# First attention: router logits taken before the output projection, and a new order of TensorE, ScalarE and GpSimd in each step

## What is computed

```python
x = x + tanh(g_xattn[0]) * xattn0(layernorm(x), ctx, ctx, w_q, b_q, w_k, b_k, w_v, b_v, w_o, b_o)
# first mixture: xn = (x - mu) / sqrt(var + eps) * gamma + beta
logits = xn @ Wg.T + bg            # 8 experts, the best 2 of them per token
x = x + tanh(g_ffn[0]) * (layernorm(x) + sum over 2 experts of w * expert(xn))
```

## Time and profile before

| what | value |
|---|---|
| median of 3 runs | 1355.66 us (1352.38 to 1358.79) |
| the profiled execution | 1369.84 us, its span 1368.0 us |
| mean granted TensorE clock | 0.981 |
| busy in the span | PE 95%, DVE 68%, ACT 58%, POOL 52% |
| chain that ended last | PE 85%, DVE 8%, DMA 3%, ACT 2% |

### The profile page before, as it was taken

One profiled execution on the slowest core, in us unless ns is written; L12 is line 12 of the kernel. 1 busy time (PEld: TensorE's weight loads), 2 busy tenths in 40 slices (PEclk: granted clock), 3 DMA queues, 4 the chain that ended last, 5 costly groups with the idle time before them and its releaser, 6 DMA issues.

```text
span 1368.0 us, 38200 instructions
## 1 busy us (share of the span) xinstructions
PE 1297.2 (95%) x14802; PEld 1154.4 (84%) x14802; DVE 930.5 (68%) x2484; ACT 794.5 (58%) x1761; POOL 712.2 (52%) x708
## 2 busy tenths in 40 slices
PE   6999999998889999999999998999999999899898
PEld 5888888886789999999999986889999998545476
DVE  4788888897576655556556216999999997412287
ACT  4566666663457777777777444666566665332454
POOL 1365656553266877778877024566665652200131
PEclk9999999999899999999999997999999999999999
DMA  6574545463457777776775921541121110499812
GB/s 196 186 246 157 182 146 182 148 202 98 158 178 215 221 227 225 232 227 220 221 224 190 375 80 33 174 164 48 53 60 48 49 41 17 172 429 432 355 56 70
DMA packets 103618, 237.24 MB, mean 173 GB/s; under 512 B 8976, under 2 KB 85904, under 8 KB 91024
## 3 DMA queue, kind: packets, MB, share of 16 engines
q1 hardware_dynamic: 97296, 218.02, 46.3%
q0 software_dynamic: 6144, 16.79, 3.9%
HBM read 173.96 MB, written 60.82 MB: 172 GB/s over the span
## 4 chain that ended last, share of the span: by engine, by line
PE 85%; DVE 8%; DMA 3%; issue 2%; ACT 2%; POOL 0%; SPq 0%; DVEq 0%; ACTq 0%; PEldq 0%; POOLq 0%
PE ps L1542 13%; PE psT L1527 7%; PE ps L598 5%; PE psS L575 5%; PE ps L802 5%; PE ps L750 4%; PE psT L584 4%; PE psS L1527 3%; PE ps L1527 3%; PE ps L611 3%; PE ps L735 2%; PE ps L764 2%; PE ps L674 2%; PE psT L590 2%; PE ps L1780 2%
## 5 line engine op out<-in xcount | busy, mean ns | idle before, releaser
L1495 POOL TENSOR_TENSOR wb_lo<-arena,wb_hi 128x2048 fp32r<-128x2048 f32 x64 | 298.0, 4657 | 104.4 <-ACT wb_hi L1615 104.4
L1542 PE MATMUL ps<-wb_hi,hT_hi 128*128 128x256 f32 x528 | 153.3, 290 | 6.5 <-DVE hT_lo L1668 6.5
L584 PE MATMUL psT<-arena 32*128 32x128 f32 x2048 | 155.3, 286 | 0.0
L1542 PE MATMUL ps<-wb_lo,hT_hi 128*128 128x256 f32 x528 | 148.6, 281 | 0.0
L1542 PE MATMUL ps<-wb_hi,hT_lo 128*128 128x256 f32 x528 | 148.6, 281 | 0.0
L575 PE MATMUL psS<-arena 32*128 32x256 f32 x1024 | 143.2, 397 | 0.7 <-ACT arena L963 0.7
L1615 ACT CAST wb_hi<-arena 128x1024 fp32r<-128x1024 f32 x128 | 130.6, 1044 | 6.5 <-DMA arena<-w_dram 6.2
L1169 POOL TENSOR_TENSOR arena<-arena,eps_sb 128x1 f32<-128x1 f32 x96 | 26.2, 273 | 203.2 <-DVE arena L1043 115.4
L584 PEld LDWEIGHTS psT<-arena 32*128 32x128 f32 x2048 | 129.2, 188 | 2.6 <-issue 1.8
L1680 DVE TENSOR_TENSOR arena<-ps,arena 128x512 f32<-128x512 f32 (+1 forms) x39 | 25.4, 650 | 120.1 <-PE ps L1542 79.7
L1542 PEld LDWEIGHTS ps<-wb_hi,hT_hi 128*128 128x128 f32 x528 | 100.3, 190 | 6.8 <-issue 6.7
(11 more groups left out here) (385 smaller groups left out, 3894.4 us busy)
## 6 DMA issues: line engine op xcount, KB each, us to landing
arena<-wset_dram SPq DMA_DIRECT2D x24, 2048.0 KB, 15.5
xs_rows<-arena SPq DMA_DIRECT2D x33, 1024.0 KB, 8.2
arena<-w_dram SPq DMA_DIRECT2D x32, 1028.0 KB, 6.0
arena<-w_dram SPq DMA_DIRECT2D x32, 1024.0 KB, 5.9
arena<-w_dram SPq DMA_DIRECT2D x7, 2052.0 KB, 12.9
w_sb<-xs_rows SPq DMA_DIRECT2D x33, 256.0 KB, 2.7
xs_rows<-arena SPq DMA_DIRECT2D x33, 256.0 KB, 5.5
arena<-ctxT_dram SPq DMA_DIRECT2D x63, 128.0 KB, 2.4
```

What stands on the lines that cost most here:

```text
L584: nc.tensor.matmul(psT[:, b, j * P:(j + 1) * P], kbd[p, (k - 1) % 3, c, par, :], qT[p, (k - 1) % 3, c, :], start=j == 0, stop=False, skip_ ...
L1495: nc.gpsimd.tensor_tensor(wb_lo[:, u % 2, part], wb_raw[:, u % 2, part], wb_hi[:, u % 2, part], ALU.subtract).then_inc(w_g.sem, 1)
L1542: last = nc.tensor.matmul(ps[5][:, t * D:(t + 1) * D], hp[:, f, t * P:(t + 1) * P], wp[:, f, :], start=f == 0 and t == 0 and n == 0, stop= ...
```

## The change

1. **Logits without xn on TensorE.** The logits are linear in x apart from the row's mean and spread. The gate weights, times gamma, are centred over the columns (`wc`), so that the mean drops out. The part of the old x comes from a product of the turned xh (xT) with `wc` (8 columns), made behind Q; ScalarE scales it by the row's spread (`lg_x`), and GpSimd adds a constant row. The part of the attention's output comes with the output product, whose weights `wo_wide` have the 8 columns of w_o times `wc` behind the 256. VectorE adds the two (`lg_sum`) and scales by xn's factor a step later. The turn of xn, its copy by ScalarE and its product go.
2. **Setting up.** TensorE forms the column sums of the scaled gate weights before the first keys, the gate through the transposed output weights (a new load of 256 KB, `oT`) and the constant row in step 2. The gate weights are loaded with the first constants, and scaled by VectorE at once.
3. **The next input first.** The turn of xh of tile k+1 moves from behind the rank product to behind the first score half, and ScalarE copies it ahead of the keys. Q then waits for the copied values, since they share a PSUM bank.
4. **Residual's affine part.** Its two factors are made by GpSimd (from VectorE), and the pass over x by ScalarE (from VectorE), ahead of its copy of aT.
5. **Scatters a tile apart.** The first scatter of tile k-4 is issued ahead of the context parts, the second at the start of the next step, behind a wait for the transposed scores' first half.
6. In the second attention the late contexts are waited for one at a time; the bias addition to x on GpSimd moves one step later.

```diff
+        wo_wide = arena[:, wo_at:wo_at + C * (D + E0)].rearrange("p (c d) -> p c d", c=C)
+        wo_turned = w_sb[:, 3]
...
+        def gate_sums(pe):
+            pe.wait_ge(fold_v, 1)
+            for c in range(C):
+                last = nc.tensor.matmul(ps[4][:, 0:E0], ones[:, :], wc[:, c, :], start=c == 0, stop=c == C - 1)
+            last.then_inc(prep_p, 1)
+
+        def gate_centred(dve):
+            dve.wait_ge(prep_p, 1)
+            for c in range(C):
+                nc.vector.scalar_tensor_tensor(out=wc[:, c, :], in0=ps[4][:, 0:E0], scalar=-1.0 / D,
+                                               in1=wc[:, c, :], op0=ALU.mult, op1=ALU.add).then_inc(fold_v, 1)
+
+        def gate_through_output(pe):
+            pe.wait_ge(fold_v, 3)
+            for m in range(C):
+                for c in range(C):
+                    last = nc.tensor.matmul(ps[7][:, D + (1 + m) * E0:D + (2 + m) * E0], wo_turned[:, c, m * P:(m + 1) * P],
+                                            wc[:, c, :], start=c == 0, stop=c == C - 1)
+            last.then_inc(prep_p, 1)
...
+        def gate_biases(pe):
+            pe.wait_ge(fold_v, 4)
+            pe.wait_ge(setup_v, 6)
+            for c in range(C):
+                nc.tensor.matmul(ps[7][:, 0:E0], xn_columns[:, c, :], wo_wide[:, c, D:D + E0],
+                                 start=c == 0, stop=False)
+            for c in range(C):
+                last = nc.tensor.matmul(ps[7][:, 0:E0], xn_columns[:, 2 * C + c, :], wc[:, c, :],
+                                        start=False, stop=c == C - 1)
+            last.then_inc(prep_p, 1)
...
 def tensor(pe)
+                def input_turned(i):
+                    pe.wait_ge(ln_v.sem, ln_v.at(i, "xh"))
+                    before(pe, pre_a.sem, pre_a.at(i - 1, "xT"))
+                    if A:
+                        before(pe, u_a.sem, u_a.at(i - 1, "u"))
...
                 if A:
-                    pe.wait_ge(ld_first, 32)
+                    gate_sums(pe)
+                    pe.wait_ge(ld_first, 48)
...
+                    if A and k == 2:
+                        gate_biases(pe)
                     scores(k, 0)
                     if A and k == 2:
-                        pe.wait_ge(setup_v, 6)
+                        pe.wait_ge(fold_v, 5)
+                    if A and valid(k + 1):
+                        input_turned(k + 1)
...
-                    if A and valid(k - 3):
-                        pe.wait_ge(n2_v.sem, n2_v.at(k - 3, "xn"))
-                        before(pe, av_a.sem, av_a.at(k - 2, "av"))
-                        before(pe, rk_v.sem, rk_v.at(k - 4, "run") if valid(k - 4) else 0)
-                        for c in range(C):
-                            last = nc.tensor.transpose(ps[4][:, c * P:(c + 1) * P], xn[:, (k - 3) % 3, c * P:(c + 1) * P],
-                                                       cv["ident"])
-                        last.then_inc(rt_p.sem, 1)
...
                         pe.wait_ge(pre_a.sem, pre_a.at(k + 1, "xT"))
+                        if A and k + 1 >= early:
+                            pe.wait_ge(kv_a.sem, kv_a.at(k + 1, "V"))
...
-                    if A and valid(k - 3):
-                        pe.wait_ge(rt_a.sem, rt_a.at(k - 3, "xnT"))
...
-                            last = nc.tensor.matmul(ps[5][:, D:D + E0], xnT[:, c, :], wg_sb[:, c, :],
-                                                    start=c == 0, stop=c == C - 1)
+                            last = nc.tensor.matmul(ps[5][:, D:D + E0], xT[:, c, :], wc[:, c, :], start=c == 0, stop=c == C - 1)
...
-                                last = nc.tensor.matmul(ps[7][:, D:2 * D], aT[:, c, :], wo[:, c, :],
+                                last = nc.tensor.matmul(ps[7][:, 0:D + E0], aT[:, c, :], wo_wide[:, c, :],
...
 def scalar(act)
+                    if A and valid(k + 1):
+                        act.wait_ge(pre_p.sem, pre_p.at(k + 1, "xT"))
+                        before(act, pre_p.sem, pre_p.at(k, "x"))
+                        nc.scalar.copy(xT.rearrange("p c t -> p (c t)"), ps[5][:, 0:D]).then_inc(pre_a.sem, 1)
                     if valid(k + 1) and stashed(k + 1):
...
                     if A and valid(k - 3):
-                        act.wait_ge(rt_p.sem, rt_p.at(k - 3, "xnT"))
-                        nc.scalar.copy(xnT.rearrange("p c t -> p (c t)"), ps[4][:, 0:D]).then_inc(rt_a.sem, 1)
+                        act.wait_ge(n2_g.sem, n2_g.at(k - 3, "shift"))
+                        act.wait_ge(n2_v.sem, n2_v.at(k - 3, "xn"))
+                        nc.scalar.activation(x_all[:, k - 2], x_all[:, k - 2], ACT.Identity, bias=rs[:, 1:2], scale=rs[:, 0:1])\
+                            .then_inc(n2_a.sem, 1)
...
+                        nc.scalar.activation(lg_x[:, (k + 1) % 4, :], ps[5][:, D:D + E0], ACT.Identity, bias=0.0,
+                                             scale=spread[:, (k + 1) % 4:(k + 1) % 4 + 1]).then_inc(u_a.sem, 1)
...
 def vector(dve)
-                        nc.vector.tensor_scalar(rs[:, 0:1], rq[:, 0:1], tg[:, 2:3], 1.0, ALU.mult, ALU.add)\
-                            .then_inc(n2_v.sem, 1)
-                        nc.vector.tensor_scalar(rs[:, 1:2], mv[:, 1, 0:1], tg[:, 2:3], rq[:, 0:1], ALU.mult, ALU.mult)\
-                            .then_inc(n2_v.sem, 1)
...
-                        dve.wait_ge(rt_p.sem, rt_p.at(rt_i, "lg"))
-                        nc.vector.tensor_tensor(lg, ps[5][:, D:D + E0], bg_sb[:, :], ALU.add).then_inc(rt_v.sem, 1)
+                        dve.wait_ge(out_v.sem, out_v.at(rt_i, "t"))
+                        nc.vector.scalar_tensor_tensor(out=lg, in0=lg_sum, scalar=rq[:, 1:2], in1=bg_sb[:, :],
+                                                       op0=ALU.mult, op1=ALU.add).then_inc(rt_v.sem, 1)
...
+                            nc.vector.scalar_tensor_tensor(out=lg_sum, in0=ps[7][:, D:D + E0], scalar=tg[:, 0:1],
+                                                           in1=lg_x[:, out_i % 4, :], op0=ALU.mult, op1=ALU.add)\
+                                .then_inc(out_v.sem, 1)
...
-                        nc.vector.tensor_scalar(x_all[:, ln_i + 1], x_all[:, ln_i + 1], rs[:, 0:1], rs[:, 1:2],
-                                                ALU.mult, ALU.subtract).then_inc(n2_v.sem, 1)
...
 def gpsimd(pool)
+                        nc.gpsimd.tensor_tensor(spread[:, i % 4:i % 4 + 1], rstd[:, j, 0:1], rstd[:, j, 1:2], ALU.mult)\
+                            .then_inc(t.sem, 1)
...
+                    if A and valid(k - 5):
+                        if valid(k - 1):
+                            pool.wait_ge(st_p.sem, st_p.at(k - 1, "a"))
+                        scatter(k - 5, 1)
+                    if A and valid(k - 3):
+                        pool.wait_ge(n2_g.sem, n2_g.at(k - 3, "rstd"))
+                        before(pool, n2_a.sem, n2_a.at(k - 4, "res"))
+                        nc.gpsimd.tensor_scalar(rs[:, 0:1], rq[:, 0:1], tg[:, 2:3], 1.0, ALU.mult, ALU.add).then_inc(n2_g.sem, 1)
+                        nc.gpsimd.tensor_scalar(rs[:, 1:2], mv[:, 1, 0:1], ntg, rq[:, 0:1], ALU.mult, ALU.mult)\
+                            .then_inc(n2_g.sem, 1)
...
+                        pool.wait_ge(u_a.sem, u_a.at(k - 2, "u"))
+                        nc.gpsimd.tensor_tensor(lg_x[:, (k - 2) % 4, :], lg_x[:, (k - 2) % 4, :], lg_row, ALU.add)\
+                            .then_inc(bias_g.sem, 1)
...
+                    if A and valid(k - 4):
+                        pool.wait_ge(zeroed[k % 2], dma_at(k - 4, k % 2))
+                        if valid(k - 1):
+                            pool.wait_ge(st_p.sem, st_p.at(k - 1, "b"))
+                        pool.wait_ge(rk_v.sem, rk_v.at(k - 4, "put"))
+                        scatter(k - 4, 0)
```

More of the change, by code:

```diff
@@ L640, in ahead_values @@
                     last.then_inc(stash_p, 1)
+                def input_turned(i):
[3 more added lines that the diff above has]
+                        before(pe, u_a.sem, u_a.at(i - 1, "u"))
+                    else:
+                        before(pe, x1_v.sem, x1_v.at(i - 6, "V"))
+                        before(pe, x2_v.sem, x2_v.at(i - 7, "mask"))
+                    for c in range(C):
+                        last = nc.tensor.transpose(ps[5][:, c * P:(c + 1) * P], xh[:, (i) % 2, c * P:(c + 1) * P],
+                                                   cv["ident"])
+                    last.then_inc(pre_p.sem, 1)
                 if A:
-                    pe.wait_ge(ld_first, 32)
+                    gate_sums(pe)
+                    pe.wait_ge(ld_first, 48)
                     pe.wait_ge(ld_kv, 16)
@@ L2148, in vector @@
                                         cv["parity"][:, None, :].to_broadcast([P, C, 2]), ALU.mult).then_inc(setup_v, 1)
+                for c in range(C):
+                    last = nc.vector.tensor_scalar(wc[:, c, :], wg_sb[:, c, :], col["gamma"][:, c:c + 1], None, ALU.mult)
+                last.then_inc(fold_v, 1)
```

154 lines of the change are left out of this document (90 added, 64 removed).

## The result

| | before | after |
|---|---|---|
| median (9 runs each) | 1362.53 us (1352.38 to 1368.37) | 1350.45 us (1342.02 to 1356.75) |
| profiled execution, its span | 1369.84, 1368.0 us | 1347.85, 1346.1 us |

The ratio is 0.992, 95% interval 0.9891 to 0.9949. The change makes the kernel 12.1 us faster; the forecast was 15.8 less, and a median of 1339.9. The three runs of before that stood in front of the forecast (median 1355.66) lay low: the nine have 1362.53.

What follows compares the result with a forecast made beforehand. TensorE was taken as the bound, VectorE close behind. Steady steps -9.6, start -1.9 and tail -4.3 sum to -15.8 us, from a median of 1355.66 to 1339.9; own range 1332 to 1347, chance 0.58.

Steps and rivals of the forecast that it cites:

- Steady steps: First attention, steps 4 to 30: net gain 0.34 us a step with the ring, 0.38 without, 9.6 us in all.
- the wait for xn: TensorE, each steady step: xn's turn and the wait for it go, 0.66 us with the ring, 0.70 without.
- the ring: Steps 8 to 23, where the first expert's weights are also split; step forecast at 9.37 us, 9.2 without.
- rival one: More is won: parted scatters give 2.9 us, a Q that doesn't wait 7.8; median 1329; chance 0.12.
- VectorE: Steady steps: 0.5 us less work a step (0.3 to 0.6), own path 8.7, under TensorE's 9.37.
- GpSimd: Steady steps: four small ops add 1.1 us to 6.0; with scatter issue it stands at 7.7 of 9.4.
- rival three: GpSimd becomes the bound, scatters taking over twice 1.01 us: step 0.5 longer, +7.3 us, 1363; chance 0.04.
- Start: Kernel's start: new products and later landing against vanished waits and clock fall, together -1.9 us (-4.5 to +3).
- the late Q: Start, steps 0 to 3: Q no longer waits for an xT copied last, some 0.8 us won by estimate.
- the new products and the later landing: Start: gate sums, output-weight and bias products 1.9 us, later landing and VectorE 0.6: +2.5 (+1 to +4).
- the fall of the clock near 48: Start, 48 to 55 us: low clock loses 2.8 us; expected gone with two chances in three, -1.8.
- Tail: Steps 31 to 34: xn's wait and turn go, exponential waited for instead; -4.3 us (-2 to -6).
- Behind the first attention: Second attention keeps its order, late contexts waited for one by one under loads issued long before: 0.

Runs made afterwards that it cites:

- e3: The kernel before with only the two scatters of a tile parted into different steps: 1359.15 us, ratio 1.0006 to the kernel before.
- e13: Changed kernel with the logits product ahead of Q and the residual's affine pass back on VectorE: 1342.12 us, ratio 0.9875 to the kernel before.
- e1: The changed kernel again, no edit: 1348.44 against 1359.74 us for the kernel before, ratio 0.9938.
- e15: The changed kernel unedited, on another chip: 1347.41 us, ratio 0.9907 to the kernel before.
- e5: The kernel before again, unaltered, as a control: 1363.91 against 1362.97 us, ratio 1.0013.
- e11: Changed kernel with both scatters of a tile in a row at the end of GpSimd's step: 1343.23 us (4 runs), ratio 0.9864 to the kernel before.
- e2: Changed kernel with the logits product ahead of Q's wait for the copied values: 1345.89 us, ratio 0.9912 to the kernel before.
- e8: Changed kernel with the residual's affine pass back on VectorE, its factors still on GpSimd: 1348.9 us, ratio 0.9896 to the kernel before.
- e14: Changed kernel with logits ahead of Q, residual's pass on VectorE, and first scatter waiting for VectorE's maxima: 1342.78 us, ratio 0.9879 to the kernel before.
- e12: Changed kernel with logits first, scatter waiting for maxima, xh made by ScalarE, gate's sums behind first values: 1347.18 us, ratio 0.9909 to the kernel before.
- e7: Changed kernel with the gate's sums behind the first keys and values, gate weights on a later semaphore: 1346.03 us, ratio 0.9878 to the kernel before.
- e9: Changed kernel with logits ahead of Q and the first scatter waiting for VectorE's split maxima: 1346.72 us, ratio 0.9907 to the kernel before.

## Why the forecast was right or wrong

The direction of the change and the mechanism of the steady steps were right. The median came out at 1350.45, 10.5 us above 1339.9. That is outside the forecast's own range of 1332 to 1347, and just inside the 1328 to 1351 that the rivals span. (By the bounds that it names, those of start and tail, the own range begins at 1335.6 and not at 1332.) 6.9 of the 10.5 is the base: the forecast was made from 1355.66, the median of three runs, and the median of nine is 1362.53. The other 3.7 is the change: 12.1 in place of 15.8 less. (On the other chips it was 11.3 and 14.1.) The term of the sum that failed is the start: -1.9 was booked and +1.3 measured. By parts:

- **Steady steps: right, and a little small.** Forecast 9.6 us for 27 steps, so 8.9 for the 25 of the table above. They went from 242.0 to 230.8 us, 11.2 less. The terms: the wait for xn is gone; Q waits 0.29, as worked out; steps without the ring are 9.22 (forecast 9.2). Ring steps are 9.22 too, not 9.37. That is rival one's first half, to which I gave too little: parting the scatters takes the ring's 0.18 out, as e3 shows alone. Its other half, a Q that doesn't wait, did not come.
- **VectorE: wrong in size, without a price here.** I expected 0.5 us less a step. 141.11 us in 152/9.22 = 16.5 steps are 8.56, and before it was 137.16/16.1 = 8.52. What it lost went into clashes with GpSimd. In the mean of the ring's steps the cast of the experts' indices takes 0.44 for 0.17, the logits' sum 0.42 for 0.21 and the maxima's second cast 0.33 for 0.17. Against that, the one clash that the forecast had seen, the cast of the places (0.45 in the mean before), is gone: 0.17. In the changed kernel nobody waits for them; in e13, with ScalarE out of the way, the step does. The Trainium skill ("SBUF — State Buffer", section "SBUF: two separate sides") says that VectorE and GpSimd share a port pair under an exclusive lock; whoever starts first holds it for the whole instruction, VectorE where it works in a two-port mode or reads two inputs from SBUF. The trace after agrees where the slowed cast ends at 202.52 and the scatter at 202.54. It doesn't agree where a cast that starts 0.11 into a scatter keeps its 0.17, and there the measurement decides; the last section has more of them.
- **GpSimd: right.** 119.31/16.5 = 7.2 us busy a step, forecast 7.1 and with the issue 7.7; rival three did not come.
- **Start: the step that failed.** Forecast -1.9. Between executions whose start had no fall of the clock (e3's 59.2 with the start of the kernel before, e1's 60.5 and e15's 60.4) it is +1.3. TensorE of e3, then of e1:

```profile
18.65 1.16 PE L750 MATMUL ps<-arena,w_sb 128*128 128x128 f32 x8 [0.85 <-ACT arena L924]
...
45.29 0.44 PE L720 MATMUL ps<-const,arena 128*128 128x128 f32 x2 [1.51 <-DVE arena L1061]
```

```profile
19.98 1.13 PE L802 MATMUL ps<-arena,w_sb 128*128 128x128 f32 x8 [0.88 <-ACT arena L899]
...
23.35 1.04 PE L424 MATMUL ps<-arena,w_sb 128*128 128x8 f32 x8
24.32 0.49 PE L625 MATMUL psS<-arena 32*128 32x256 f32 x2
...
32.88 0.61 PE L437 MATMUL ps<-arena 128*128 128x8 f32 x4
...
33.87 0.48 PE L625 MATMUL psS<-arena 32*128 32x256 f32 x2
```

  The wait for xn (1.51) did go: the step that held it is 10.74 in e3 and 9.22 in e1. Three terms were wrong. First, *the late Q*: 0.8 was booked because Q would no longer wait for xT. Q waits 0.85, 0.59 and 0.22 in steps 0 to 2 of e3 and 0.88, 0.62 and 0.25 in e1, now for the copied values (L899). It is the wait that the forecast itself put into the steady steps and left out here. Second, *the new products and the later landing* were put at 2.5 and cost 3.4: TensorE begins 0.53 later, the sums take 0.88, the gate through the output weights 0.97 and the biases 0.99. Of that 0.2 falls under waits: 3.1 by the averages of tile 1, which with the 1.5 of xn's wait and 0.3 of step 4, a steady one, leaves the +1.3. Third, *the fall of the clock near 48*, for which I took 1.8 off, is not a property of the kernel before: e5 and e3 don't have it. Falls come at other places from one execution to the next; the changed kernel had one of 10.2 us at 22 in its own profile (the 0.50 in the windows above) and none in e1 and e15.
- **Tail: right.** Forecast -4.3. With the same 10.2 us at low clock it is 53.8 before and 49.3 in e15: -4.5, of which 0.3 is one more steady step. No wait of 1.25 for xn is left; TensorE waits for exponentials instead, as forecast, and also for the copies of aT (0.46 at 310.54). Two lines of the tail after, in steps 31 and 32:

```profile
308.31 0.48 PE L625 MATMUL psS<-arena 32*128 32x256 f32 x2 [0.50 <-ACT arena L955]
...
316.11 1.16 PE L634 MATMUL psT<-arena 32*128 32x128 f32 x16 [0.41 <-ACT arena L955]
```

- **Behind the first attention: nothing**, as assumed: 1003.7 and 1008.3 us before, 1002.9 to 1005.0 after.

These parts sum to -11.2 + 1.3 - 4.5 = -14.4 us. That the forecast's -15.8 lies so near is in part luck: the steps gave 2.3 more than forecast, and the start 3.2 less. The medians say -11 to -14, and not all of that has a place in the code. A kernel's runs are some 1 us longer for each 0.001 of mean clock that they miss. The 20 runs of the changed kernel have a mean clock of 0.9834, those of the kernel before 0.9806 (83 runs, on the chips of e1 to e15), so by estimate 3 us of the medians' difference go with the clock, and no run shows whether the change brings that. The parts compare executions or stretches alike in clock as far as they could be had, so 4 us or so of them don't show in the medians and stay unexplained. What stays open too is how the pair of scatters stretches TensorE's first score half by 0.26 in ring steps of the kernel before. e11 shows that the place matters, but the rows name no wait.

**Why a step stopped at 9.22** took the longest, and the forecast did not see it. Two paths end a step there. TensorE's own work, with Q's wait in it, comes to the maxima's transpose at 9.07 after the averages, and the next averages follow 0.15 later. ScalarE's chain (keys, values, residual, aT, exponential, Q copies) lets the transpose go at 8.96, and behind such a wait the averages follow 0.24 later: 9.20. The forecast asked of ScalarE whether aT and the exponential come in time, and they do; it left out that Q's copies stand behind them, and that the maxima use Q's bank. With one path relieved (e2, or e8) the other holds at 9.2. With both relieved it is 9.12, held by VectorE (e13), and with the scatter moved as well 9.03 (e14).

## What to carry to other kernels

When a relief brings nothing, look at the waiting instruction's other semaphores in the code, and at when each releaser ended in the timeline; the list of waits names only one of those that end close together. Two paths of nearly equal length need both reliefs in one kernel: e2 and e8 brought nothing to the step alone, 0.1 together, and 0.2 with the scatter out of VectorE's way. A wait that is booked in one stage belongs in the sum of every stage that has the same order: Q's wait for the values stood in the steady steps and was missing in the start. And don't book the end of a clock fall as a gain from one profile: look whether a second execution of the same kernel has it.

## What the runs showed of the hardware

Of two scatters of the same length one held VectorE's cast of 16 columns (0.74 us) and one did not (0.17): the cast that began 0.32 us into it was held to its end, the one that began at 0.11 was not. In the 17 traces, from 96 to 300 us, 364 such casts begin beside a scatter. The 238 that begin up to 0.31 us into it all take 0.17 to 0.20. The 107 that begin 0.36 us in or later all end 0.02 to 0.03 us before the scatter does. The 19 between go either way. So in these traces a scatter costs such a cast nothing in its first 0.3 us, and up to 0.6 us after that.

VectorE's reduction of 1024 columns from PSUM kept its 1.22 us in both kernels, beside whatever GpSimd did.

The granted clock was at 0.5 for 26 to 57 us of each execution, at places that differ between executions of one kernel, but never in the 25 steady steps, where TensorE is busy all along. Apart from that TensorE's first products take double their time, and until when differs: to 9.7 us in e12, 13.5 in e1, 18.4 in e7, 22.4 in e13 and e14, whose granted clock reads 1.00 all the while. TensorE of e14:

```profile
18.87 1.92 PE L661 MATMUL ps<-arena,w_sb 128*128 128x128 f32 x8
20.57 1.91 PE L672 MATMUL ps<-w_sb,arena 128*128 128x256 f32 x4
```

By this the profiled start of e14 is 64.4 us, 4.0 longer than e15's. The order of its code is not what does it: e9, with the logits first as well, has 60.0. Of e13's and e14's profiles only the steps were compared above, not their spans.
